# The last batch's second layer by token tiles, with b2 added by TensorE

## The reference, cut to what matters

```python
h = _ln(_ln(x, pw_g[pathway], pw_b[pathway]), cp_g[comp], cp_b[comp])
t = _ln(x, tm_g[time], tm_b[time]);  s = _ln(x, ms_g[scale], ms_b[scale])
m, n, r = (x + _mlp_ln(state, ...)[:, None, :] for each of three states)
cat = jnp.concatenate([w[0]*h, w[1]*t, w[2]*m, w[3]*n, w[4]*r, w[5]*s], axis=-1)
out = x + _mlp_ln(cat, int_W1, int_b1, int_W2, int_b2, int_g, int_be)
# _mlp_ln(s, ...) = _ln(silu(s @ W1 + b1) @ W2 + b2, g, be)
```

## Time and profile before

| what | us |
|---|---|
| median of 3 runs | 1016.01 (1015.41 to 1016.51) |
| profiled execution, its own time | 1013.07 |
| its span | 1011.4 |
| TensorE busy in the span | 966.6 (96%) |
| VectorE busy | 805.1 (80%) |
| GpSimd busy | 515.5 (51%) |
| ScalarE busy | 267.7 (26%) |

### The profile page before, as it was taken

The page is one execution under the profiler, slowest core; times in us unless marked ns, Lnnn a source line. Parts: engine busy times, 40 slices in busy tenths (PEclk is TensorE's granted clock), DMA queues, the critical chain, the costliest instruction groups (busy, mean ns, idle before and its releaser), DMA issues.

```text
span 1011.4 us, 13658 instructions
## 1 busy us (share of the span) xinstructions
PE 966.6 (96%) x4404; PEld 796.4 (79%) x4404; DVE 805.1 (80%) x1109; ACT 267.7 (26%) x330; POOL 515.5 (51%) x619
## 2 busy tenths in 40 slices
PE   0998999999999999999999999999999999999994
PEld 0776788888888888888888888888888888888883
DVE  6687879788787978879697887869788787978844
ACT  4233223232232323223232322323232232323120
POOL 4343537455463745547374554637455563744311
PEclk9999999999999999999999999999999999999997
DMA  9764454446355443635444363554436355443121
GB/s 331 227 253 157 136 145 128 139 99 206 84 170 141 134 138 91 207 84 186 125 141 135 86 207 83 179 132 145 133 85 203 87 175 136 147 131 85 43 62 41
DMA packets 52786, 142.19 MB, mean 141 GB/s; under 512 B 10233, under 2 KB 10505, under 8 KB 48673
## 3 DMA queue, kind: packets, MB, share of 16 engines
q0 software_dynamic: 23168, 66.60, 26.3%
q1 hardware_dynamic: 29600, 75.37, 21.5%
HBM read 125.04 MB, written 16.91 MB: 140 GB/s over the span
## 4 chain that ended last, share of the span: by engine, by line
PE 93%; DVE 3%; POOL 2%; DMA 1%; issue 1%; DVEq 0%; POOLq 0%; SPq 0%
PE hid_ps L1182 23%; PE hid_ps L1184 23%; PE hid_ps L1183 23%; PE o_ps L1263 5%; PE o_ps L1264 5%; PE o_ps L1262 5%; PE made_ps L1162 3%; PE made_ps L1175 3%; PE hid_ps L1187 1%; DMA token_stats<-x_pack 1%; DMA x_sb<-x 0%; DVE xst L716 0%; PE o_ps L1102 0%; PE o_ps L1139 0%; POOL xrs L407 0%
## 5 line engine op out<-in xcount | busy, mean ns | idle before, releaser
L1182 PE MATMUL hid_ps<-cat_hi,w_hi 128*128 128x512 f32 x1024 | 403.4, 394 | 27.9 <-POOL w_lo L485 24.2
L1184 PE MATMUL hid_ps<-cat_hi,w_lo 128*128 128x512 f32 x1024 | 400.0, 391 | 0.0
L1183 PE MATMUL hid_ps<-cat_lo,w_hi 128*128 128x512 f32 x1024 | 399.8, 390 | 0.0
L1182 PEld LDWEIGHTS hid_ps<-cat_hi,w_hi 128*128 128x128 f32 x1024 | 193.2, 189 | 68.6 <-issue 25.0
L1184 PEld LDWEIGHTS hid_ps<-cat_hi,w_lo 128*128 128x128 f32 x1024 | 192.9, 188 | 40.6
L1183 PEld LDWEIGHTS hid_ps<-cat_lo,w_hi 128*128 128x128 f32 x1024 | 193.3, 189 | 39.2
L467 POOL DMA_INDIRECT pw_rows<-cp,class_now x64 | 127.7, 1996 | 81.9 <-DVE y_sb L791 71.6
L604 ACT ACTIVATE cat_hi<-v_ring 128x1024 fp32r<-128x1024 f32 x64 | 68.0, 1063 | 313.1 <-DVE v_ring L773 313.1
L460 POOL DMA_INDIRECT pw_rows<-pw,path_now x64 | 97.0, 1516 | 63.4 <-DVE y_sb L809 42.3
L405 POOL TENSOR_TENSOR fve<-fmv,eps_col 128x1 f32<-128x1 f32 x64 | 39.8, 622 | 157.4 <-DVE fmv L828 157.4
L481 POOL DMA_DIRECT2D r_sb<-x x60 | 57.7, 962 | 105.5 <-DVE r_sb L857 94.8
(11 more groups left out here) (128 smaller groups left out, 1194.5 us busy)
## 6 DMA issues: line engine op xcount, KB each, us to landing
x_sb<-x SPq DMA_DIRECT2D x16, 1024.0 KB, 6.5
xc<-xT SPq DMA_DIRECT2D x16, 1024.0 KB, 5.1
out<-r_sb SPq DMA_DIRECT2D x64, 256.0 KB, 2.0
r_sb<-x POOLq DMA_DIRECT2D x60, 256.0 KB, 4.7
stats_bc<-token_stats SPq DMA_DIRECT2D x30, 256.0 KB, 5.0
ids_sb<-ids SPq DMA_DIRECT2D x16, 256.0 KB, 7.4
keep<-int_W SPq DMA_DIRECT2D x12, 256.0 KB, 6.7
w_raw<-int_W SPq DMA_DIRECT2D x12, 256.0 KB, 10.8
```

The lines of the kernel that those rows point to most:

```text
L1182: pe.matmul(acc, w1_hi[:, k, cols], hi, start=start, stop=False)
L1183: pe.matmul(acc, w1_hi[:, k, cols], lo, start=False, stop=False)
L1184: return pe.matmul(acc, w1_lo[:, k, cols], hi, start=False, stop=stop)
```

## The change

The second layer of batch 15 no longer goes block by block over all quarters, but quarter by quarter: all four `last_pairs` come first, and then for each quarter one matmul that adds b2 and the twelve matmuls of its four blocks. The added matmul multiplies a 128 x 128 block of ones (in `onehot`) by a 128 x 512 array that is zero but for two rows (in `scaled`): row 0 the high part of b2, row 32 the low part. GpSimd makes both behind its last `add_x`: two memsets, two casts of one row, one subtraction, announced by a semaphore `b2_ready`, for which TensorE waits ahead of the first of these matmuls. VectorE's `last_stats` takes the place of `out_stats` there: statistics and (o - mean) * g are read from PSUM directly, and the copy with b2 is gone.

```diff
+            pool.wait_ge(filled, 6 * (BATCHES - 1) + FT)
+            pool.wait_ge(used, 6 * (BATCHES - 1) + 1)
+            pool.memset(scaled[:, :].bitcast(f32), 0.0).then_inc(b2_cleared, 1)
+            pool.memset(onehot[:, 0:P].bitcast(f32), 1.0).then_inc(b2_cleared, 1)
+            pool.wait_ge(b2_cleared, 2)
+            for at in (0, 32):
+                pool.tensor_copy(scaled[at:at + 1, :], b2_bc[at:at + 1, :]).then_inc(b2_rounded, 1)
+            pool.wait_ge(b2_rounded, 2)
+            pool.tensor_tensor(scaled[32:33, :], b2_bc[32:33, :], scaled[32:33, :].bitcast(f32),
+                               ALU.subtract).then_inc(b2_ready, 1)
+            pool.wait_ge(b2_ready, 1)
             for t in range(TT):
                 out_rstd(BATCHES - 1, t)
...
+            def last_stats(t):
+
+                n = TT * (BATCHES - 1) + t + 1
+                dve.wait_ge(second_done, n)
+                dve.bn_stats(fst[:, t, :], last_ps[t]).then_inc(fstat, 1)
+                dve.wait_ge(fstat, n)
+                dve.nop(nofuse=True)
+                dve.bn_aggr(fmv[:, t, :], fst[:, t, :]).then_inc(faggr, 1)
+                dve.wait_ge(faggr, n)
+
+                dve.wait_ge(out_ready, n - 2)
+                dve.scalar_tensor_tensor(o_sb[:, t % 2, :], last_ps[t], fmv[:, t, 0:1], g_bc,
+                                         ALU.subtract, ALU.mult).then_inc(fnum, 1)
...
             for t in range(TT):
-                out_stats(BATCHES - 1, t, last_ps[t])
+                last_stats(t)
                 if t > 0:
                     last_sum(t - 1)
...
-            def last_second(k):
-                pe.wait_ge(last_lo_done, k + 1)
-                for t in range(TT):
-                    if k == 0 and t == 0:
-                        pe.wait_ge(h_lo_done, 2 * BATCHES)
-                    if k == 0 and t >= 2:
-                        pe.wait_ge(o_done, TT * (BATCHES - 1) + t - 3)
-                    cols = slice(t * P, (t + 1) * P)
-                    pe.matmul(last_ps[t], hid_hi[:, k, cols], w2_hi[:, k, :], start=(k == 0), stop=False)
+            def last_second(t):
+
+                if t >= 2:
+                    pe.wait_ge(o_done, TT * (BATCHES - 1) + t - 3)
+                cols = slice(t * P, (t + 1) * P)
+                if t == 0:
+                    pe.wait_ge(b2_ready, 1)
+                pe.matmul(last_ps[t], onehot[:, 0:P], scaled[:, :], start=True, stop=False)
+                for k in range(FT):
+                    if t == 0:
+                        pe.wait_ge(last_lo_done, k + 1)
+                    pe.matmul(last_ps[t], hid_hi[:, k, cols], w2_hi[:, k, :], start=False, stop=False)
...
-                    if k == FT - 1:
-                        ins.then_inc(second_done, 1)
+                ins.then_inc(second_done, 1)
...
-                if not last:
-                    for h in range(FT):
-                        last_pairs(b, h)
-                else:
-                    for h in range(FT - 1):
-                        last_pairs(b, h)
-                    last_second(0)
-                    last_pairs(b, FT - 1)
-                    for k in range(1, FT):
-                        last_second(k)
+                for h in range(FT):
+                    last_pairs(b, h)
+                if last:
+                    for t in range(TT):
+                        last_second(t)
```

More of the change, by code:

```diff
@@ L246, in build @@
         x_offset = sem("x_offset")
+        b2_cleared = sem("b2_cleared")
+        b2_rounded = sem("b2_rounded")
+        b2_ready = sem("b2_ready")
         second_done = sem("second_done")
```

## The result

| | before | changed |
|---|---|---|
| median | 1015.74 us (4 executions, 1015.41 to 1016.51) | 1007.77 us (4 executions, 1007.46 to 1008.44) |
| profiled execution | 1013.07 us, span 1011.4 | 1007.69 us, span 1006.0 |
| ratio | | 0.9921, 95% interval 0.9904 to 0.9939 |

The change makes the kernel faster, as forecast, but the time lies 1.7 us under the forecast of 1009.5 us and 0.5 us under the range. The medians differ by 8.0 us, the spans of the two traces by 5.4 us, and the sum of the prediction was 6.5 us. These three numbers are what has to be brought together.

What follows compares the result with a forecast made beforehand. TensorE's matmuls were taken to bound the kernel (93% of the chain), leaving a 15 us tail to win. Terms -7.65, +0.91, +0.15 and +0.1 gave -6.49 us, so 1016.01 - 6.5 = 1009.5 us, range 1008.3 to 1011.9.

Steps and rivals of the forecast that it cites:

- the sum of the prediction: Total over the tail: -7.65 at the mark, +0.91 and +0.15 on TensorE, +0.1 at the end, together -6.49 us.
- TensorE's order and the b2 matmuls: Second layer's tail: reordering adds no matmuls; four b2 matmuls at 0.227 us add 0.91 us, at most 1.56.
- the mark: Start of the fourth quarter's statistics, 1004.09 us before; to fall from 8.08 to 0.43 us behind TensorE's last matmul.
- The hidden block: Hidden block 3, now covered by ten matmuls or 2.27 us, makes TensorE wait 0.15 us (bounds 0 and 0.4).
- b2 from GpSimd: GpSimd's memsets, casts and subtraction have b2 ready at 983.97 us, before TensorE wants it at 985.13; price nothing.
- The rule of the Trainium skill: VectorE with two SBUF inputs and a GpSimd instruction reading SBUF exclude each other for the whole instruction.
- the rival of a late block: GpSimd's three reads held by VectorE, 2.07 us added, b2 late by 0.7 to 2.4 us: 1011.1 us, chance 0.18.
- the cover: Margin of 1.2 us between b2 being ready and TensorE wanting it; past it each microsecond counts in full.
- VectorE: Per quarter 2.57 us without the copy, against TensorE's 2.95, so VectorE waits; reading PSUM in statistics and scaling costs 0.
- The rival of slow PSUM reads: Statistics and scaling from PSUM take 1.4 us more, VectorE 3.97 us a quarter: 1013.9 us, chance 0.04.
- The end: Behind the fourth quarter's statistics start, 7.31 us before: +0.1 us as a sum may meet GpSimd's root (bounds -0.2, +0.3).
- the best case: Lower end with b2 in time: 1008.4 us, with the end's -0.2, no block 3 wait, half a microsecond's spread.

Runs made afterwards that it cites:

- e_slowb2: The changed kernel with four more one-row GpSimd casts, each awaited, before b2 is ready: 1009.84 us, ratio 0.9949.
- n_after: The changed kernel run again without any edit: 1007.3 us, ratio 0.9934, span 1004.5.
- e_b2: The kernel before with b2 added on TensorE only, keeping the order block by block: 1010.98 us, ratio 0.9974.
- e_tiles: The kernel before with the order by quarters only, VectorE still adding b2 in its copy: 1008.86 us, ratio 0.9946.
- e_sum: The changed kernel with all four b2 matmuls ahead of the first quarter's products and each sum behind its own statistics: 1007.53 us, ratio 0.9933.
- e_best: The two moves of e_sum plus ten matmuls filling TensorE's wait near 82 us, on the changed kernel: 1006.78 us, ratio 0.9924.
- n_after2: The changed kernel run once more without any edit: 1006.7 us, ratio 0.9930, executions from 1005.25 to 1009.04 us.

## Why the prediction was right and wrong

**TensorE's order and the b2 matmuls: right.** The pitch of the b2 matmul is 0.23 us. Before, 21.68 us lay between the last matmul of `last_pairs` for h = 2 and the mark (982.41 to 1004.09); in the changed kernel, with the twelve matmuls for h = 3 counted back (2.72 us from 986.61), it is 983.89 to 999.02, 15.13 us. The mark came 6.55 us earlier; the terms for it add up to 6.59.

**The hidden block: right.** From the last matmul's start to the low part it took 2.51 us (986.61 to 989.12), against 2.50. The gap it left in TensorE is 0.18 us (989.51 - 988.88 is 0.63, where two pitches are 0.45), against 0.15.

**b2 from GpSimd: right in its end, not in its parts.** The timeline of the changed kernel:

```profile
980.48 0.89 POOL L484 DMA_DIRECT2D r_sb<-x  x1 [1.39 <-DVE r_sb L886]
...
982.12 1.70 POOL L574 CAST scaled<-rows_bc 1x512 fp32r<-1x512 f32 x2
...
982.26 2.11 DVE L849 TENSOR_TENSOR hid_lo<-z_sb,hid_hi 128x512 fp32r<-128x512 f32 x2
...
983.90 1.61 POOL L576 TENSOR_TENSOR scaled<-rows_bc,scaled 1x512 fp32r<-1x512 f32 x1
```

From the issue of the last DMA to the end of the block it is 5.03 us, against 4.96 reckoned. The two casts took 1.70 us as a pair (2.18 reckoned) and the subtraction 1.61 us (1.09), so two errors cancel. The two low parts beside the casts took 2.11 us as a pair, where one takes 0.69: they were held for 0.7 us. Both engines waited in turn, VectorE with work that was not urgent. The rule of the Trainium skill that the prediction names ("SBUF — State Buffer", "Who interferes with whom") agrees with the rows of `e_slowb2`: of two that overlap, the one that starts first keeps its time (0.61 us for the cast at 987.14), and the other is held, by some 0.35 us, also where GpSimd works on one row. The `hid_lo` of 987.27 us was held for 0.33 us, less than the 0.48 us that the cast is listed to last from there, so the rows show who waits, but not that the wait is for the whole instruction. As for the rival of a late block: its mechanism is real but small. Against their times in `e_slowb2` with nothing of VectorE beside them (0.60 and 1.26 us), the two casts (0.68 and 0.96 us) and the subtraction were held for 0.8 us together, where the rival reckoned 2.07 and more. With that included b2 was still 1.1 us ahead of TensorE; what lateness past the cover costs is what `e_slowb2` shows.

**VectorE: right.** Statistics 0.70 us and scaling 0.75 us out of PSUM, as out of SBUF (0.69 and 0.78); VectorE waits ahead of each quarter (1.05, 1.19, 0.52 and 0.52 us). The rival of slow PSUM reads is excluded.

**The end: mis-sized by 0.45 us.** I charged +0.1 us behind the mark and expected 7.3 to 7.5 us there. It is 6.98 us (999.02 to 1006.0) and 6.96 (`n_after`), against 7.31: -0.35. VectorE's own part is the same, 3.10 and 3.11 us, although the root now takes 0.55 us instead of 0.86 beside the scaling. The rest lies behind the last sum, 3.9 us against 4.2, and there no row tells what it is. `e_b2` has 3.9 us too, `e_tiles` 4.2, `e_sum` and `e_best` 4.3; in all of them the last store's transfer ends 1.7 to 1.8 us behind the last sum, so the difference lies behind the stores. The cause stays open.

**The step that failed: from the sum to the median.** The prediction took 6.5 us off the median of three executions, 1016.01 us, said that this stands 2.9 us above the profiled one, and gave it a spread of half a microsecond. In the changed kernel the distance is 0.1 us to its own profiled execution (1007.77 against 1007.69), which had the clock low near 84 us, and 1.6 us to that of `n_after` (1006.21), which had not. The 84 executions say what the 2.9 us were: the three lay where the upper of two groups does (1014.7 to 1016.5) and the profiled one in the lower (1012.1 to 1013.9). The spread of this kernel is over 4 us (1012.1 to 1016.5), and three executions that happened to agree hid it. The distance between the executions shown and the profiled one was a question to ask, not a constant to carry over. Of the 1.7 us by which the forecast missed, 0.45 is the end, and 0.3 is the base, whose median became 1015.74 with a fourth execution. The remaining 1 us is the draw, as far as that can be said of a remainder: a kernel with two groups was measured in its upper one before, and after in executions whose clock (0.995, 1007.5 to 1008.4 us) stood low for a shorter time than in the worst of its group (0.993, 1009.0). The measured 8.0 us are thus 7 us of the change and 1 us of the draw, within the interval of 6.2 to 9.8.

**Two slips in the sums.** The lower bound for b2 by the terms given is 980.66 + 3 x 0.52 + 0.04 = 982.3 us, not 982.8; and the best case is 1009.5 - 0.3 - 0.15 - 0.5 = 1008.55 us, not 1008.4. The outcome hangs on neither.

## What to carry to other kernels

When work is spread over tiles that all get ready at the end, finish one tile after the other on the bound engine, and the engine behind it works off all but the last while matmuls run. Moving 0.72 us of VectorE's work per tile onto TensorE for 0.23 us pays where VectorE is the slower of the two per tile. Before a forecast is set on a median, compare the profiled execution with it: if they differ by more than the executions differ among themselves, the kernel may have groups, and the range has to hold the distance.

## What the runs showed of the hardware

Behind a wait of TensorE of 2.6 us near 84 us the granted clock was at its lower level in four traces (the changed kernel, `n_after2`, `e_tiles` and `e_slowb2`), for 3.4 us in three and for 6.8 us in `e_slowb2`; in the other unfilled traces, with the same wait, it stayed at 1.00. By times and mean clocks, 41 of 84 executions of one kernel lay near 1015.4 us and 43 near 1013.1. With ten matmuls in the wait the upper group was gone in all 32 executions (22 of the kernel before, 10 of the changed one and of `e_best`), while every unfilled kernel measured had executions in its upper group. For the kernel before no trace shows the fall itself.

On GpSimd a 1x512 cast took 0.60 us and a 1x512 subtraction 1.26 us alone, and 0.95 and 1.61 us beside a VectorE instruction that reads two SBUF operands. That VectorE instruction then took 1.02 to 1.10 us instead of 0.69. A 128x512 subtraction took 1.40 us on average, so one row instead of 128 saved little there.
